# Row maxima of a graph attention layer: written to DRAM in two pieces, read back over 128 partitions, running maxima turned in contiguous blocks

## The chip, the cores and the metric

The kernel runs on one core of one Trainium2 chip. The metric is the device time of one execution in microseconds (us); lower is better.

## The reference, cut to what matters

For each of 8 graphs of N = 1500 nodes and 64 features, an attention layer with 4 heads comes first, and then three light layers with layer norms between them.

```
scores = einsum('hbnd,hbdm->hbnm', f_self, f_other)      # 4 heads, 1500 x 1500 each
masked = a * scores;  masked = where(masked >= 0, masked, 0.2 * masked) / sqrt(16)
masked = masked + where(a == 0, -1e9, 0)
attn   = softmax(masked, axis=-1)
x = layernorm(x + relu(attn @ feats + bias))
x = layernorm(x + (adj + I) @ x / degree)
x = layernorm(x + adj @ (x @ w2) + bias2)
t = adj @ x;  x = layernorm(x + where(t > 0.5, 1, 0))
```

The softmax over a row of 1500 needs the row's maximum before any of its exponentials can be taken. The change touches only how these maxima travel.

## The kernel before, in words

P = 125 nodes stand on the partitions, 12 tiles of them make the 1500. C = 500 is a slice of rows (ST = 4 nodes to a partition), and there are 3 slices. A unit is one graph, one pair of heads and one slice: 48 units, u = 0 to 47, six to a graph. A unit has 12 steps, one for each tile of 125 neighbours, so there are 576 steps q, and every engine runs through one loop over q in which each job has a fixed offset.

In step q, TensorE fills a PSUM tile Z (125 neighbours by 2 heads by 500 rows: two matmuls at L496 with the mask, two at L498 with the scores). ScalarE bends it with the leaky function into LS (L677). VectorE keeps the running maximum RUN over the steps (L820 in a unit's first step, L823 in the others). The neighbours lie on the partitions, so after 12 steps RUN still has 125 candidates for each of the 1000 maxima. One step later the unit's maxima are finished and spread, in this order:

1. TensorE transposes RUN in eight matmuls (turn_run, L509, one for each of 2 heads and 4 groups of 125 rows). PE's order in that step is fixed: the turn comes ahead of the next fill of Z.
2. VectorE reduces the turned tile to RMAX, 125 x 8 (row_maxima, L829).
3. ScalarE bends it into LMAX (L692).
4. The SyncE queue (SP) writes LMAX to a DRAM row of 1000 numbers, `spread` (the tensor row_maxima, L303), waits until that has landed, and reads the row back into MB on all 125 partitions (L309). MB and `spread` have two buffers each, for u even and odd. The same queue issues the feature copies (L286, 24 in a batch, two batches to a graph) and the loads and stores of x.

The subtraction of the maxima runs 18 steps behind the fill (LAG): POOL does two steps of three (L403), VectorE every third (L837), and POOL's first one of a unit waits for MB. POOL's next pair waits for VectorE's one. Two steps behind the subtraction ScalarE takes the exponential (L685), and two behind that TensorE multiplies by the values V (L535). LS holds 24 steps; the fill of a new one needs an old one to have been weighed.

Between these, in steps fixed by hand, stand the turns of the adjacency (L552: three transposes, each of a contiguous block of 125 words), the light layers of the graph before (L586 and L596 on TensorE, L905 to L940 on VectorE, L408 and L412 on POOL) and the features of the next one.

Of the kernel before, what the change touches and what calls it, by code (L numbers as in the profile page):

```python
# [8 lines left out]
P = 125  # L9
NT = N // P  # L10
ST = 4
NS = NT // ST
C = ST * P
# [55 lines left out]
def adj_resnorm(nc, x, adj, wv, wself, wother, bias0, w2, bias2, out):  # L69
    f32, bf16, f16, f8 = mybir.dt.float32, mybir.dt.bfloat16, mybir.dt.float16, mybir.dt.float8e4  # L70
    ALU, ACT, AX = mybir.AluOpType, mybir.ActivationFunctionType, mybir.AxisListType
# [6 lines left out]
    spread = nc.dram_tensor("row_maxima", (2, 2 * C), f32).ap()  # L78

    ctx = ExitStack()  # L80
    with ctx:
        def sb(name, shape, dt):
            return ctx.enter_context(nc.sbuf_tensor(name, shape, dt))

        def sem(name):
            return ctx.enter_context(nc.semaphore(name))
# [5 lines left out]
        LS = sb("LS", [128, RL, 2, C], f32)  # L92
        V = sb("V", [P, 2, NT, H, VC], f32)
        RUN = sb("RUN", [P, 2, 2, C], f32)
        MB = sb("MB", [P, 2, 2, C], f32)
        PARTS = sb("PARTS", [128, 3, N], bf16)
        YT = sb("YT", [128, C], f32)
        REST = sb("REST", [128, C], f32)
# [18 lines left out]
        LMAX = sb("LMAX", [P, 2, 2 * ST], f32)  # L117
# [5 lines left out]
        ID = sb("ID", [128, 128], f32)  # L123
# [23 lines left out]
        max_out = [sem(f"max_out{i}") for i in range(2)]  # L147
        mb_in = [sem(f"mb_in{i}") for i in range(2)]
        sub_pool = sem("sub_pool")
        sub_dve = sem("sub_dve")  # L150
# [49 lines left out]
        def unit_at(q, at):  # L200

            u, off = divmod(q - at, STEPS)
            return u if off == 0 and 0 <= u < NU else None

        def graph_at(q):
            return divmod(q, SPG)
# [60 lines left out]
        def banks(*what):  # L267
            return Z[:, place[what] % RZ, :, 0:C]

        def link_of(b, l, n):  # L270

            return LINKS * b + 3 * l + n + 1

        def by_pool(e):

            return e // TURN * (TURN - 1) + min(e % TURN, TURN - 1)


        @block.sync
        def _(sp):  # L280
            def load_rows(b, dst, sem_):
                sp.dma_start(dst.rearrange("p (s k) f -> p s k f", k=ST), x_v[b]).then_inc(sem_, 16)

            def load_parts(dst, sem_, side, h):
                for n, pair in enumerate(TERMS):
                    sp.dma_start(dst[n * D:(n + 1) * D],  # L286
                                 PARTS[side * F + h * D:side * F + (h + 1) * D, pair[side], :]).then_inc(sem_, 16)

            def load_features(b, p):
                sp.wait_ge(lo_ready, NS * (b + 1))  # L290
                if b >= 1:

                    sp.wait_ge(z_full, SPG * (b - 1) + NS * STEPS * (p + 1))
                for h in (2 * p, 2 * p + 1):
                    load_parts(FO[:, h, :], fo_in[p], 1, h)
                    load_parts(FS[:, h, :], fs_in[p], 0, h)

            def spread_maxima(u):
                sp.wait_ge(max_bent, u + 1)
                if u >= 2:  # L300

                    sp.wait_ge(mb_in[u % 2], 16 * (u // 2))
                sp.dma_start(spread[u % 2].rearrange("(h i c) -> i h c", i=P, c=ST),  # L303
                             LMAX[:, u % 2, :].rearrange("p (h c) -> p h c", c=ST)).then_inc(max_out[u % 2], 16)
                sp.wait_ge(max_out[u % 2], 16 * (u // 2 + 1))
                if u >= 2:
                    sp.wait_ge(sub_pool, by_pool(STEPS * (u - 1)))
                    sp.wait_ge(sub_dve, STEPS * (u - 1) // TURN)
                sp.dma_start(MB[:, u % 2, :, :].rearrange("p h c -> p (h c)"),  # L309
                             spread[u % 2].partition_broadcast(P)).then_inc(mb_in[u % 2], 16)  # L310

            load_rows(0, XF, xf_in)
            sp.dma_start(WA[:, 0, :, :], wself.rearrange("h f o -> f h o")).then_inc(early_in, 16)
            sp.dma_start(WA[:, 1, :, :], wother.rearrange("h f o -> f h o")).then_inc(early_in, 16)
            sp.dma_start(WV[:, :, :], wv.rearrange("h f o -> f h o")).then_inc(early_in, 16)
            load_features(0, 0)
            load_features(0, 1)
            sp.dma_start(WW[0:F, 1, :], w2).then_inc(weights_in, 16)
            sp.dma_start(WW[F:2 * F, 1, :], w2).then_inc(weights_in, 16)
            sp.dma_start(B0[:, :, :].rearrange("p h o -> p (h o)"),  # L320
                         bias0.rearrange("a b h o -> (a b h o)").partition_broadcast(P)).then_inc(weights_in, 16)
            sp.dma_start(B2[:, :], bias2.partition_broadcast(P)).then_inc(weights_in, 16)
            load_rows(0, XA[:, :, :], xa_in)
            for q in range(END):
                b, r = graph_at(q)
                if unit_at(q, MAX_AT) is not None:
                    spread_maxima(unit_at(q, MAX_AT))
                if r == 1 and 1 <= b < B:
                    load_features(b, 1)
                if r == 11 and b + 1 < B:  # L330
                    if b >= 2:

                        sp.wait_ge(dve_seq, link_of(b - 2, 3, 2))
                    load_rows(b + 1, XF, xf_in)
                if r == 13 and b >= 2:
                    sp.wait_ge(x_ready, 4 * (b - 1))
                    sp.dma_start(out_v[b - 2], X[:, :, :].rearrange("p (s k) f -> p s k f", k=ST)).then_inc(stored, 16)
                if r == 29 and 1 <= b < B:
                    sp.wait_ge(dve_seq, link_of(b - 1, 0, 1))
                    load_rows(b, XA[:, :, :], xa_in)  # L340
                if r == 37 and b + 1 < B:
                    load_features(b + 1, 0)
            for c in range(NS):
                sp.wait_ge(end_x, 9 + c + 1)
                sp.dma_start(out_v[B - 1][:, c], X[:, ST * c:ST * (c + 1), :]).then_inc(stored, 16)
            for p in range(PAIRS):
                sp.wait_ge(fs_in[p], 16 * 2 * NF * B)
                sp.wait_ge(fo_in[p], 16 * 2 * NF * B)
            sp.wait_ge(stored, 16 * (B - 1) + 16 * NS)
# [3 lines left out]
        def _(pool):  # L353
# [40 lines left out]
            def subtract(e):  # L394
                u, c = divmod(e, STEPS)
                if c == 0:
                    pool.wait_ge(mb_in[u % 2], 16 * (u // 2 + 1))
                if e % TURN == 0:

                    pool.wait_ge(sub_dve, e // TURN)  # L400
                pool.wait_ge(bent, e + 1)
                rows = LS[:P, e % RL, :, :]
                nc.gpsimd.tensor_tensor(rows, rows, MB[:, u % 2, :, :], ALU.subtract).then_inc(sub_pool, 1)  # L403

            def power(b, l):

# [57 lines left out]
        def _(pe):  # L464
# [37 lines left out]
            def turn_run(u):  # L502

                pe.wait_ge(maxed, STEPS * (u + 1))
                ring_free(place["RT", u])
                z = banks("RT", u)
                for hh in range(2):
                    for c in range(ST):
                        last = nc.tensor.transpose(z[:P, hh, c * P:(c + 1) * P], RUN[:, u % 2, hh, c:C:ST], ID[:P, :P])  # L509
                last.then_inc(run_turned, 1)  # L510

            def degrees(u):
# [137 lines left out]
            for l in range(3):  # L650
                for q in range(NS):
                    pe.wait_ge(end_low, 3 * l + q + 1)
                    for c in range(NS):
                        if l and q == 0:
                            pe.wait_ge(end_taken, 3 * (l - 1) + c + 1)
                        for m in range(ST * q, ST * (q + 1)):
                            last = nc.tensor.matmul(Z[:, c, 0, 0:C], XP[:, m, :], AT[:P, (NS * (B - 1) + c) % RS, q, :, m % ST],  # L657
                                                    start=(m == 0), stop=(m == NT - 1))
                        if q == NS - 1:
                            last.then_inc(end_y, 1)  # L660
                for c in range(NS):
# [3 lines left out]
                    for k in range(ST):  # L665
                        last = nc.tensor.matmul(Z[:P, c, 1, k * F:(k + 1) * F], parts[c][:, k * P:(k + 1) * P],
                                                WW[:, 1 if l == 1 else 0, :], start=True, stop=True)
# [4 lines left out]
        def _(act):  # L672
# [14 lines left out]
            def bend_maxima(u):  # L687

                act.wait_ge(max_found, u + 1)
                if u >= 2:  # L690
                    act.wait_ge(max_out[u % 2], 16 * (u // 2))
                nc.scalar.activation(LMAX[:, u % 2, :], RMAX[:, u % 2, :], ACT.Prelu, alpha=0.2).then_inc(max_bent, 1)  # L692

            def take(u):
# [109 lines left out]
        def _(dve):  # L804
# [28 lines left out]
            def subtract(e):  # L833
                u, c = divmod(e, STEPS)
                dve.wait_ge(mb_in[u % 2], 16 * (u // 2 + 1))
                rows = LS[:P, e % RL, :, :]
                nc.vector.tensor_tensor(rows, rows, MB[:, u % 2, :, :], ALU.subtract).then_inc(sub_dve, 1)  # L837

            def keep_adj(g, k, bank):
                dve.wait_ge(a_turned, ST * g + k + 1)  # L840
# [108 lines left out]
            for q in range(END):  # L949
# [12 lines left out]
                if feature_at(q) and feature_at(q)[0] == "FT":  # L962
                    _, bb, c = feature_at(q)
# [16 lines left out]
                if 0 <= e < QN and e % TURN == TURN - 1:  # L980
                    subtract(e)
# [99 lines left out]
```

## Time and profile before

| | |
|---|---|
| median of 3 runs | 1768.12 us (1765.34 to 1771.2) |
| the profiled execution's own time | 1762.62 us |
| its span | 1760.8 us |
| mean granted TensorE clock | 0.912 |
| busy: PE, DVE, ACT, POOL | 1454.2, 1384.5, 1241.6, 1089.5 us |

The span runs from the first to the last instruction of the profiled execution. PE is TensorE's matmuls and PEld its weight loads, DVE is VectorE, ACT ScalarE, POOL GpSimd, SP SyncE. A busy share is not a bound by itself: the engines hand tiles to one another, and the chain of waits tells which work stood last at each moment.

### The profile page before, as it was taken

What the parts mean: (1) busy time and instruction counts of PE and PEld (TensorE: products, weight loads), DVE (VectorE), ACT (ScalarE), POOL (GpSimd) and SP (SyncE); (2) the same over time, 40 slices, a digit from 0 to 9 for tenths busy, and PEclk for the clock granted to TensorE, in tenths of its full rate; (3) what the DMA queues carried; (4) which work ended last, traced back from release to release, by engine and by line L of the source; (5) the groups of instructions that cost most, each with busy time, mean ns of one, the idle gap of its engine ahead of it and who ended that gap; (6) DMA issues with size and microseconds to landing.
All of it is one profiled execution on the core that took longest, in us unless ns stands there. A gap on an engine that the chain in (4) does not pass through costs nothing.

```text
span 1760.8 us, 22052 instructions
## 1 busy us (share of the span) xinstructions
PE 1454.2 (83%) x7728; PEld 718.8 (41%) x7728; DVE 1384.5 (79%) x1623; ACT 1241.6 (71%) x1475; POOL 1089.5 (62%) x581
## 2 busy tenths in 40 slices
PE   4487889898889889888889888988899987888745
PEld 3233334444444444444444443444444443344313
DVE  3567788878898778888888778987888788888654
ACT  2377878777687777777787777777687777777521
POOL 1056676676676666676576667776666766766642
PEclk9788989999899999999999999999999999999767
DMA  5413142122413133221522234130432214000000
GB/s 77 61 32 48 31 66 40 46 30 39 70 31 46 26 52 51 52 36 26 68 40 43 25 55 58 39 44 17 63 46 52 30 37 55 21 12 24 15 6 9
DMA packets 55067, 71.42 MB, mean 41 GB/s; under 512 B 21814, under 2 KB 42814, under 8 KB 54958
## 3 DMA queue, kind: packets, MB, share of 16 engines
q0 software_dynamic: 13824, 18.01, 13.7%
q1 hardware_dynamic: 41134, 52.01, 11.4%
q8 instruction: 62, 1.02, 0.3%
q14 instruction: 47, 0.39, 0.1%
HBM read 102.29 MB, written 3.26 MB: 60 GB/s over the span
## 4 chain that ended last, share of the span: by engine, by line
PE 45%; DVE 24%; issue 12%; ACT 11%; SPq 3%; POOL 3%; DMA 2%; ACTq 0%; POOLq 0%; DVEq 0%
PE M L586 11%; DVE RUN L823 9%; PE M L535 9%; PE Z L496 8%; PE Z L498 7%; ACT LS L677 6%; PE Z L509 4%; DVE LS L837 4%; ACT LS L685 3%; SPq L286 2%; DVE X L922 2%; POOL LS L403 2%; PE Z L596 2%; DVE RUN L820 2%; PE Z L657 2%
## 5 line engine op out<-in xcount | busy, mean ns | idle before, releaser
L403 POOL TENSOR_TENSOR LS<-LS,MB 125x1000 f32<-125x1000 f32 x384 | 894.7, 2346 | 489.4 <-DVE LS L837 334.8
L823 DVE TENSOR_TENSOR RUN<-Z,RUN 125x1000 f32<-125x1000 f32 x528 | 631.0, 1195 | 208.7 <-ACT LS L677 203.4
L677 ACT ACTIVATE LS<-Z 125x1000 f32<-125x1000 f32 x576 | 574.5, 998 | 262.0 <-PE Z L498 261.4
L685 ACT ACTIVATE LS<-LS 125x1000 f32<-125x1000 f32 x576 | 594.5, 1033 | 71.3 <-POOL LS L403 56.2
L496 PE MATMUL Z<-AT,BI 126*125 126x500 fp8e4 x1152 | 386.0, 418 | 140.1 <-DVE RUN L823 107.0
L535 PE MATMUL M<-LS,V 125*18 125x500 f32 x2304 | 326.7, 642 | 57.8 <-ACT LS L685 57.0
L498 PE MATMUL Z<-FS,FO 96*125 96x500 bf16 x1152 | 360.1, 395 | 0.0
L837 DVE TENSOR_TENSOR LS<-LS,MB 125x1000 f32<-125x1000 f32 x192 | 283.2, 1475 | 4.9 <-DMA MB<-row_maxima 2.8
L496 PEld LDWEIGHTS Z<-AT,BI 126*125 126x125 bf16 x1152 | 140.7, 146 | 282.9 <-DVE RUN L823 164.5
L498 PEld LDWEIGHTS Z<-FS,FO 96*125 96x125 bf16 x1152 | 165.5, 144 | 111.4 <-issue 21.3
L586 PE MATMUL M<-AT,XP 125*128 125x500 fp8e4 x756 | 206.8, 396 | 0.7 <-ACTq L735 0.7
L586 PEld LDWEIGHTS M<-AT,XP 125*128 125x128 f16 x756 | 63.6, 98 | 169.6 <-issue 106.8
L509 PE MATMUL Z<-ID,RUN 125*125 125x125 f32 x384 | 99.9, 407 | 26.8 <-DVE RUN L820 24.1
L535 PEld LDWEIGHTS M<-LS,V 125*18 125x18 f32 x2304 | 39.6, 98 | 185.4 <-issue 101.7
L509 PEld LDWEIGHTS Z<-ID,RUN 125*125 125x125 f32 x384 | 91.5, 323 | 46.3 <-DVE RUN L820 39.9
L365 POOL DMA_DIRECT2D A<-in_adj_dram x96 | 53.7, 560 | 85.9 <-PE Z L552 58.7
L820 DVE TENSOR_SCALAR RUN<-Z 125x1000 f32<-125x1000 f32 x48 | 57.3, 1193 | 47.8 <-DMA B<-in_L_gnn_bias_dram 30.0
L829 DVE TENSOR_REDUCE RMAX<-Z 125x8 f32<-125x1000 f32 x48 | 57.3, 1194 | 26.1 <-PE Z L509 26.1
L596 PEld LDWEIGHTS Z<-WW,YT 128*125 128x125 f32 x504 | 63.9, 190 | 28.7 <-issue 22.0
L922 DVE SCALAR_TENSOR_TENSOR X<-Y,RSTD 125x768 f32<-125x768 f32 x28 | 72.4, 2585 | 3.6 <-POOL RSTD L408 2.4
L596 PE MATMUL Z<-WW,YT 128*125 128x64 f32 x504 | 64.7, 272 | 3.7 <-DVE RUN L820 3.7
L552 PEld LDWEIGHTS Z<-ID,A 125*125 125x125 f32 x276 | 45.8, 215 | 53.5 <-issue 28.5
(118 smaller groups left out, 1039.6 us busy)
## 6 DMA issues: line engine op xcount, KB each, us to landing
MB<-row_maxima SPq DMA_DIRECT2D x48, 488.3 KB
A<-in_adj_dram POOLq DMA_DIRECT2D x96, 183.1 KB, 4.8
FO<-PARTS SPq DMA_DIRECT2D x192, 46.9 KB, 2.1
FS<-PARTS SPq DMA_DIRECT2D x192, 46.9 KB, 2.1
XP<-in_x_dram SPq DMA_DIRECT2D x8, 375.0 KB
XA<-in_x_dram SPq DMA_DIRECT2D x8, 375.0 KB
out_dram<-X SPq DMA_DIRECT2D x7, 375.0 KB
row_maxima<-LMAX SPq DMA_DIRECT2D x48, 3.9 KB
```

The source lines that it names most:

```text
L403: nc.gpsimd.tensor_tensor(rows, rows, MB[:, u % 2, :, :], ALU.subtract).then_inc(sub_pool, 1)
L496: nc.tensor.matmul(z[:P, hh, :], BI[:, :], AT[:, g % RS, quarter, :, k], start=True, stop=False)
L498: last = nc.tensor.matmul(z[:P, hh, :], FO[:, 2 * p + hh, m * P:(m + 1) * P], FS[:, 2 * p + hh, s * C:(s + 1) * C], start=False, stop=True)
L509: last = nc.tensor.transpose(z[:P, hh, c * P:(c + 1) * P], RUN[:, u % 2, hh, c:C:ST], ID[:P, :P])
L535: last = nc.tensor.matmul(M0[VW * n:VW * n + VC, 0:C], V[:, b % 2, e % STEPS, 2 * p + hh, :], LS[:P, e % RL, hh, :], start=(p == 1 and j = ...
L586: last = nc.tensor.matmul(M1[:, 0:C], XP[:, m, :], AT[:P, (NS * b + c) % RS, m // ST, :, m % ST], start=(m == 0), stop=(m == NT - 1))
L596: last = nc.tensor.matmul(z[:P, 0, k * F:(k + 1) * F], YT[:, k * P:(k + 1) * P], WW[:, 1 if l == 1 else 0, :], start=True, stop=True)
L677: nc.scalar.activation(LS[:P, q % RL, :, :], banks("Z", q)[:P], ACT.Prelu, alpha=0.2).then_inc(bent, 1)
L685: nc.scalar.activation(rows, rows, ACT.Exp, scale=0.25).then_inc(exps, 1)
L823: nc.vector.tensor_tensor(run, z, run, ALU.max).then_inc(maxed, 1)
L837: nc.vector.tensor_tensor(rows, rows, MB[:, u % 2, :, :], ALU.subtract).then_inc(sub_dve, 1)
L922: nc.vector.scalar_tensor_tensor(out=X[:, :, :], in0=Y[:, :, :], scalar=F ** 0.5, in1=RSTD[:, :].unsqueeze(2).to_broadcast(bc3), op0=ALU.m ...
```

## The change

The running maxima are turned in blocks of 125 neighbouring columns, where before each transpose took every fourth column. The results in PSUM then belong to rows c * 125 + i instead of 4 * i + c, and the write to DRAM puts them back in order: it goes number by number. It is issued in two DMAs, of partitions 0 to 111 and 112 to 124. The read back fills 128 partitions of MB, of which 125 are used as before. The waits on the write's semaphore count 32 for each unit where they counted 16.

```diff
-        MB = sb("MB", [P, 2, 2, C], f32)
+        MB = sb("MB", [128, 2, 2, C], f32)
...
-                sp.dma_start(spread[u % 2].rearrange("(h i c) -> i h c", i=P, c=ST),
-                             LMAX[:, u % 2, :].rearrange("p (h c) -> p h c", c=ST)).then_inc(max_out[u % 2], 16)
-                sp.wait_ge(max_out[u % 2], 16 * (u // 2 + 1))
+
+                for rows in (slice(0, 112), slice(112, P)):
+                    sp.dma_start(spread[u % 2].rearrange("(j i) -> i j", i=P)[rows], LMAX[rows, u % 2, :],
+                                 allow_slow_non_contiguous=True).then_inc(max_out[u % 2], 16)
+                sp.wait_ge(max_out[u % 2], 32 * (u // 2 + 1))
...
                 sp.dma_start(MB[:, u % 2, :, :].rearrange("p h c -> p (h c)"),
-                             spread[u % 2].partition_broadcast(P)).then_inc(mb_in[u % 2], 16)
+                             spread[u % 2].partition_broadcast(128)).then_inc(mb_in[u % 2], 16)
...
-                nc.gpsimd.tensor_tensor(rows, rows, MB[:, u % 2, :, :], ALU.subtract).then_inc(sub_pool, 1)
+                nc.gpsimd.tensor_tensor(rows, rows, MB[:P, u % 2, :, :], ALU.subtract).then_inc(sub_pool, 1)
...
-                        last = nc.tensor.transpose(z[:P, hh, c * P:(c + 1) * P], RUN[:, u % 2, hh, c:C:ST], ID[:P, :P])
+                        last = nc.tensor.transpose(z[:P, hh, c * P:(c + 1) * P], RUN[:, u % 2, hh, c * P:(c + 1) * P], ID[:P, :P])
...
-                    act.wait_ge(max_out[u % 2], 16 * (u // 2))
+                    act.wait_ge(max_out[u % 2], 32 * (u // 2))
```

## Rows read from the trace of the kernel before

**Rows 1.** The page's busy tenths in 40 slices of the span.

```profile
PE   4487889898889889888889888988899987888745
DVE  3567788878898778888888778987888788888654
PEclk9788989999899999999999999999999999999767
```

**Rows 2.** The chain that ended last, shares of the span by line.

```profile
by line: issue 12.2%; PE M L586 10.6%; DVE RUN L823 8.9%; PE M L535 8.6%; PE Z L496 7.7%; PE Z L498 6.7%; ACT LS L677 5.7%; PE Z L509 4.5%; DVE LS L837 4.0%; ACT LS L685 3.0%; SPq L286 2.5%; DVE X L922 2.4%; POOL LS L403 2.2%; PE Z L596 2.1
```

**Rows 3.** Turns in the timeline of PE: start us, us, instructions.

```profile
834.92 2.04 PE L509 MATMUL Z<-ID,RUN 125*125 125x125 f32 x8
801.39 2.17 PE L509 MATMUL Z<-ID,RUN 125*125 125x125 f32 x8 [0.32 <-DVE XA L867]
67.05 0.49 PE L552 MATMUL Z<-ID,A 125*125 125x125 f32 x3
63.59 0.84 PE L552 MATMUL Z<-ID,A 125*125 125x125 f32 x3
```

**Rows 4.** Weight loads and matmuls of two lines: duration ns min/median/max.

```profile
L509 PEld LDWEIGHTS Z<-ID,RUN x384: 302/325/327, 80.7 to 1643.8; 125*125 125x125 f32 x192
L552 PEld LDWEIGHTS Z<-ID,A x276: 183/188/336, 63.2 to 1493.6; 125*125 125x125 f32 x138
L552 PE MATMUL Z<-ID,A x276: 267/273/571, 63.6 to 1493.7; 125*125 125x125 f32 x138
```

**Rows 5.** Groups of instructions: busy us, mean ns, idle before and its releaser.

```profile
L403 POOL TENSOR_TENSOR LS<-LS,MB 125x1000 f32<-125x1000 f32 x384 | 894.7, 2346 | 489.4 <-DVE LS L837 334.8 <-DMA MB<-row_maxima 150.6 <-ACT LS L677 3.8
L685 ACT ACTIVATE LS<-LS 125x1000 f32<-125x1000 f32 x576 | 594.5, 1033 | 71.3 <-POOL LS L403 56.2 <-DVE LS L837 2.8
L837 DVE TENSOR_TENSOR LS<-LS,MB 125x1000 f32<-125x1000 f32 x192 | 283.2, 1475 | 4.9 <-DMA MB<-row_maxima 2.8
```

**Rows 6.** Who waited for whom, SP's queue and POOL: total us, times, longest us.

```profile
SPq L309 <- DMA row_maxima<-LMAX: 96.4, 48, 3.3
POOL LS L403 <- DMA MB<-row_maxima: 150.6, 34, 9.8
```

**Rows 7.** SP's issues, durations in ns min/median/max, and L286's landing.

```profile
L303 SPq DMA_DIRECT2D row_maxima<-LMAX x48: 251/252/431, 85.7 to 1647.1; - x48
L309 SPq DMA_DIRECT2D MB<-row_maxima x48: 259/260/267, 89.0 to 1649.2; - x48
L286 SPq DMA_DIRECT2D FS<-PARTS x192: 576/589/1857, 25.0 to 1451.7; - x192
```

**Rows 8.** The page's hardware DMA queue: packets, MB, share of 16 engines' span.

```profile
q1 hardware_dynamic: 41134, 52.01, 11.4%
```

**Rows 9.** Windows: us, busy of five engines, PEclk, DMA share, GB/s.

```profile
607.00:611.00 4.00, 3.19 (x24) 1.06 (x16) 3.85 (x5) 3.99 (x5) 3.89 (x3) 1.00 0.27 104
```

**Rows 10.** Timeline of SP, then of POOL, unit 14.

```profile
541.30 0.27 SPq L309 DMA_DIRECT2D MB<-row_maxima  x1
...
547.96 4.61 POOL L403 TENSOR_TENSOR LS<-LS,MB 125x1000 f32<-125x1000 f32 x2 [5.38 <-DMA MB<-row_maxima]
```

**Rows 11.** The chain in order of time, units 0, 2, 5 and 11: start us, us.

```profile
88.99 9.28 DMA MB<-row_maxima
...
153.54 7.61 issue
...
241.26 8.81 DMA MB<-row_maxima
...
449.78 2.41 issue
452.19 3.29 DVE LS L837
```

**Rows 12.** Timeline around the first subtractions of unit 11.

```profile
449.15 5.27 POOL L403 TENSOR_TENSOR LS<-LS,MB 125x1000 f32<-125x1000 f32 x2 [7.39 <-DMA MB<-row_maxima]
...
451.49 1.04 ACT L685 ACTIVATE LS<-LS 125x1000 f32<-125x1000 f32 x1 [3.00 <-POOL LS L403]
```

More of the change, by code:

```diff
@@ L836, in subtract @@
                 rows = LS[:P, e % RL, :, :]
-                nc.vector.tensor_tensor(rows, rows, MB[:, u % 2, :, :], ALU.subtract).then_inc(sub_dve, 1)
+                nc.vector.tensor_tensor(rows, rows, MB[:P, u % 2, :, :], ALU.subtract).then_inc(sub_dve, 1)
             def keep_adj(g, k, bank):
```

## The prediction, made before the changed kernel ran

> **What bounds the kernel now.** I read the page first. PE is busy in eight or nine tenths of nearly every slice and DVE in seven or eight [rows 1], so no engine is the bound alone. The chain of waits tells more: it passes through PE's matmuls, DVE's running maxima and ACT's steps in turn, and L509, the turn of RUN, holds 4.5% of the span in it [rows 2]. That is 0.045 x 1760.8 = 79 us, and at about 1.9 us a turn it is 41 of the 48 turns: nearly each one stands where nothing else can go on. Then I looked for the other half of the change, the way of the maxima through DRAM. POOL waits for MB 150.6 us in 34 of 48 units [rows 5, 6]. POOL has slack, so this is not a gain by itself; it becomes one where ACT's exponential then waits for POOL (56.2 us in all) [rows 5], and in a few places of the chain [rows 11].
>
> **The turn.** Eight transposes stay eight; only the operand's step changes. Today each weight load of L509 lasts 302 to 327 ns at any clock, while L552's, the same 125 x 125 f32 from neighbouring words, lasts 188 in the median [rows 4]. The load sets the pace: eight turns last 2.04 us at the full clock [rows 3], so with a last matmul of some 0.3 us the step between two is 0.25. L552's three last 0.49 us at the full clock; less one matmul of 0.27 [rows 4] that is 0.11 us a step, and eight would last 0.27 + 7 x 0.11 = 1.04 us. That saves 1.0 us a turn. At the low clock L552's three last 0.84 us, which gives 0.21 a step and some 1.9 us for eight, against the 2.17 of a turn in which the clock fell [rows 3]: 0.3 saved. PEclk is 9 in most slices [rows 1], and nearly all turns start at the full clock with about a quarter ending at the low one, so I take 0.9. On the chain this is 41 x 0.9 = 37 us. L829 (RMAX), the next fill of Z (L496) and everything behind them come that much sooner. Bounds: nothing, if the f32 transpose were paced otherwise, and 1.0 x 48 = 48 us.
>
> **The read back.** How many DMA engines carry MB? The window of unit 16 in which only MB moves shows a DMA share of 0.27 at 104 GB/s [rows 9], near 5/16. The packets say the same. Of the 41,134 on the hardware queue [rows 8] the shapes of its transfers explain 34,290 (12,000 of the maxima's write, 6,000 of MB, 6,144 feature rows, 9,000 of x in and out, 1,146 of weights and biases). The other 6,844 are one completion for each engine used, and that comes out exactly with 5 engines for the 124 transfers over 125 rows and 16 for the 389 over 16 or 64 rows: 620 + 6,224. So 125 rows go on five engines, and 128 should go on 16, as every row count divisible by 16 here does. The Trainium skill says so too (DMA: Bandwidth & Descriptors, Why a DMA increments its semaphore by 16 and not by 1): the engines are the largest number up to 16 that divides the slowest dimension, which gives 5 for 125, 16 for 128 and 112, and 13 for 13; by this count the trace agrees for 125, 16 and 64. The same page (Specifications) puts the DRAM limit of one core near 358 GB/s; by it the read would take 1.4 us, so that limit would not change the sum.
>
> The 500 KB now take 500,000 / 104,000 = 4.8 us. With each of 16 engines at the rate of the five, 333 GB/s, the 512 KB take 1.5 us: 3.3 saved. The other end is no gain: all 16 read the same 4 KB of DRAM, and no row shows more than this rate from one such place. I take 3.3, because the engines' rate looks like their own. Against that stands the issue: SP needs 0.26 us for L309 but 0.59 for a feature copy on 16 engines [rows 7], so +0.33.
>
> **The write.** Today 250 pieces of 16 bytes go out; after, 1000 of 4 bytes: 896 / 16 = 56 an engine and then 8 more, against 50 now. If a small packet costs the same, the transfer lasts as long as now. The issues are two of 0.59 instead of one of 0.25 [rows 7]: the second ends at 1.2 us after the first began, where today's ends at 0.25, so the landing comes 0.8 to 0.9 later (less than the difference, since the first piece is under way by then). SP's wait for the write is 96.4 / 48 = 2.0 us now [rows 6] and should read some 2 from the last issue. Bounds: below, +0.3; above, each of the 64 packets at the queue's mean, 0.114 x 16 x 1760.8 us / 41,134 = 0.078 us [rows 8], or 5.0 us, +5.5 with the issue. I take +0.8: today's 50 packets and their receipt fit into 2.0 us together, so a small one costs far less than the mean. SP's queue carries 1.3 us more issue a unit, 60 us in all, in a queue that is mostly waiting; the feature batches it delays by that are issued many steps ahead of their use, so this costs nothing unless a batch runs straight into a spread, where it is in the sum already.
>
> **When POOL starts.** The parts add up to -3.3 + 0.33 + 0.8 = -2.2 us from LMAX to MB, and -3.2 with the turn's 1.0. In unit 14 POOL starts 6.7 us after L309's issue [rows 10]; that should become some 3.7 (6.7 - 3.3 + 0.33). What is late next is POOL's own work: its last subtraction of the unit before, or DVE's, which frees its next pair (334.8 us of POOL's idle time are due to that [rows 5]).
>
> What of it is on the chain? I find eight places: units 0, 2 and 5 [rows 11], and the pattern of unit 11, which comes again in 29, 35, 41 and 47. In unit 11 POOL gets MB at 449.15, so that ACT waits 3.00 us for the first subtraction [rows 12] and DVE's own L837 stands in the chain after 2.41 us of nothing, lasting 3.29 us [rows 11] where its mean is 1.475 [rows 5]: it meets POOL's second subtraction. The turn's 1.0 moves all of this together, so only the 2.2 counts: 8 x 2.2 = 18 us. For the other forty units, where the chain shows no such piece, I add nothing.
>
> **The sum.** 37 + 18 = 55 us is what the chain could give. As each piece goes, another engine stands within a fraction of a us of it (DVE and PE are both near eight tenths busy [rows 1]), so I keep four fifths: 44 us. The profiled execution took 1762.6 us, which becomes 1718.6; its median stands 5.5 us above that one (1768.1), so I predict 1724 us. The remaining edits cost nothing: MB on three more partitions is the same instruction for POOL and DVE (still 125 rows), and the doubled semaphore counts add no wait.
>
> **The rivals.**
>
> *Only the turn pays (0.17).* The read of one 4 KB place does not scale to 16 engines, or the write takes what the read gives. For it: no row shows this rate; against it: the five engines show no sign of waiting for one another. Then 18 falls out: 37 x 0.8 = 30, so 1738 us.
>
> *Only the read pays (0.08).* DVE or ACT takes the turn's place in the chain at once. For it: DVE's eight tenths; against it: on PE's side the next fill of Z stands directly behind the turn. 1768 - 18 = 1750 us.
>
> *The write becomes the bound, and the kernel slower (0.07).* 1000 writes of 4 bytes, of which different engines hit neighbouring words of the same DRAM row, may cost more each. Each us by which MB comes later than today delays POOL in the 34 units in which it already waits, and ACT in most of them, some 40 us in all at 1 us over all 48. The turn's 30 us cover 0.8 us of that. So it decides from a write stage that is 2.2 + 1.0 + 0.8 = 4 us longer than my +0.8, or 4 / 64 = 62 ns a small packet beyond today's; the upper bound above, +5.5, lies just past that. At 1 us beyond it, 1768 + 40 = 1808 us. The Trainium skill speaks for this rival (DMA: Bandwidth & Descriptors, Specifications): below 512 bytes the DMA engine does a read-modify-write. But by that rule today's 16-byte pieces pay it too, within the 2.0 us, so I leave the chance low.
>
> *The clock takes it back (0.05).* PE's work shrinks by 3% (48 of 1454 us), and what PE does at the low clock costs up to 0.84 / 0.49 = 1.7 times as much [rows 3]. For it: PEclk dips wherever PE stalls [rows 1]; against it: with shorter waits it should stall less. If the low stretches grow enough to eat the gain, 1766 us, no change.
>
> **How the numbers follow.** The forecast as it stands has 0.63: 1724 us, on its own 1708 to 1742 (the turn's 37 whole or half, the read's 18 whole or nothing). For 8 times in 10 the range must take in the second case and most of the third: 1704 to 1750. Between two builds of this kernel less than 0.3% (5 us) can't be told from no change. Faster: 0.63 + 0.17 + 0.07 = 0.87, the third case giving most of its 0.08. Same: 0.06. Slower: 0.07.
>
> **What would show it right or wrong.** In the profile after: L509's loads at some 190 ns and eight turns in 1.0 to 1.1 us at the full clock; L509's share of the chain down from 4.5% to about 2.5%; three DMA issues a unit at about 0.6 us each on SP; a DMA share near 0.8 in the microsecond or two in which MB moves; POOL starting some 3.7 us after the read's issue, and its total wait for MB falling from 150.6 us to some 60; ACT's wait for POOL falling from 56 us to under 35. SP's wait for the write is the test of the fourth case: at 2 to 3 us from the first issue I am right, above 6 us I am wrong. I would also be wrong if packets of MB lasted three times as long on 16 engines, or if DVE's subtractions met POOL's in new places: L837's mean would rise above 1475 ns.

## The result, and the profile after

The changed kernel takes 1862.84 us (median of 4 runs) against 1768.03 us: a ratio of 1.054 with a 95% interval of 1.0489 to 1.0591. It is 95 us slower where I had forecast 44 us faster, and it lies outside the range of 1704 to 1750. The profiled execution was a disturbed one (1885.39 us, clock 0.875, where the undisturbed ones show 0.882 to 0.889), so below I use its waits and durations and not its span.

The groups that answer to those of before; columns as in [rows 5], the turn's as in [rows 4]:

```profile
L405 POOL TENSOR_TENSOR LS<-LS,MB 125x1000 f32<-125x1000 f32 x384 | 916.9, 2406 | 587.9 <-DMA MB<-row_maxima 294.7
L687 ACT ACTIVATE LS<-LS 125x1000 f32<-125x1000 f32 x576 | 594.3, 1033 | 220.2 <-POOL LS L405 205.6
L839 DVE TENSOR_TENSOR LS<-LS,MB 125x1000 f32<-125x1000 f32 x192 | 307.0, 1599 | 38.1 <-DMA MB<-row_maxima 35.9
```

```profile
L511 PEld LDWEIGHTS Z<-ID,RUN x384: 182/189/336, 80.8 to 1762.7; 125*125 125x125 f32 x192
L511 PE MATMUL Z<-ID,RUN x384: 270/273/573, 81.0 to 1762.8; 125*125 125x125 f32 x192
```

The turn did what it should: a load lasts 189 ns instead of 325 in the median [rows 4]. But POOL's wait for MB rose from 150.6 to 294.7 us [rows 5], and ACT's wait for POOL from 56.2 to 205.6 us. So MB comes later, not sooner. The next three answers tell which part of its way is to blame: SP's waits (as in [rows 6]), the read's issue and landing, and the chain by line (as in [rows 2]).

```profile
SPq L311 <- DMA row_maxima<-LMAX: 360.1, 48, 12.2
```

```profile
L311 SPq DMA_DIRECT2D MB<-row_maxima x48: 337/338/352, 94.9 to 1774.0; - x48
...
DMA to landing us min/median/max: 3.7/4.7/8.3
```

```profile
by line: issue 17.1%; POOL LS L405 9.4%; DMA row_maxima<-LMAX 7.2%; SPq L286 6.1%; DVE RUN L825 6.0%; ACT LS L679 5.3%; PE Z L498 4.9%; PE M L537 4.7%; PE Z L500 4.1%; PE M L588 4.1%; DMA MB<-row_maxima 3.9%; ACT LS L687 3.4%; DVE X L924 2.
```

SP waits 360.1 / 48 = 7.5 us a unit for the write, from its last issue on, where it waited 2.0 [rows 6]. The write now holds 7.2% of the chain, a line that [rows 2] did not show at all, and the turn has left the part of the line that is shown. The read is quicker than it was: it lands a median 4.7 us after its issue, and in unit 14 POOL starts 4.2 us after it (591.19 to 595.39 below), where it took 6.7 [rows 10] and I had said 3.7.

```profile
591.19 0.34 SPq L311 DMA_DIRECT2D MB<-row_maxima  x1
...
595.39 5.55 POOL L405 TENSOR_TENSOR LS<-LS,MB 125x1000 f32<-125x1000 f32 x2 [10.59 <-DMA MB<-row_maxima]
```

Where do 7.5 us go? Unit 1 shows it, in SP's timeline and then in windows (columns as in [rows 9]):

```profile
120.69 0.88 SPq L305 DMA_DIRECT2D row_maxima<-LMAX  x2
129.24 0.34 SPq L311 DMA_DIRECT2D MB<-row_maxima  x1
```

```profile
120.50:123.00 2.50, 1.70 (x8) 0.81 (x6) 2.50 (x3) 2.38 (x5) 0.86 (x1) 1.00 0.20 2
123.00:129.00 6.00, 5.61 (x33) 2.28 (x33) 4.31 (x6) 6.00 (x9) 3.74 (x2) 1.00 0.00 0
```

Both issues are out at 121.6 and their packets are gone before 123. Then for 6 us the DMA engines do nothing (share 0.00), and only at 129.2 does SP hear that the write has landed. The packets are as cheap as I had assumed: by the trace's packet records one lasts a median 9 ns, at 16 bytes before and at 4 bytes now. What costs comes behind them: from the end of the last packet to the read's issue it is a mean 0.9 us before and 5.7 us now.

The mean of 7.5 us hides two sizes. In 13 units the write stands directly behind a batch of feature copies in SP's queue. Six of these (11, 17, 23, 29, 35 and 41) wait 9.4 to 12.3 us; the other 42 units wait a mean of 7.0. The chain shows one of the six:

```profile
465.57 0.59 SPq L286
...
466.26 0.53 SPq L305
466.79 0.04 issue
466.83 11.74 DMA row_maxima<-LMAX
```

In the 13 units SP is also late for the write itself: LMAX has been ready for 2.5 to 5.4 us while SP still issues a batch (in 14 units before, for 1.1 to 5.2 us).

### The profile page after: what moved, and what is told of

The parts are those of the page before. It is cut to its first block, busy times and chain, and to the rows that moved or that the text cites. A ratio compares the mean times of both kernels' runs of the same rounds, so it can differ in the third digit from the quotient of the medians.

```text
span 1883.6 us, 22100 instructions
## 1 busy us (share of the span) xinstructions
PE 1463.5 (78%) x7728; PEld 694.1 (37%) x7728; DVE 1405.7 (75%) x1623; ACT 1243.2 (66%) x1475; POOL 1112.2 (59%) x581
## 3 DMA queue, kind: packets, MB, share of 16 engines
q1 hardware_dynamic: 78958, 52.60, 13.7%
## 4 chain that ended last, share of the span: by engine, by line
PE 26%; DVE 18%; issue 17%; DMA 12%; ACT 11%; POOL 10%; SPq 7%; ACTq 0%; POOLq 0%; DVEq 0%
POOL LS L405 9%; DMA row_maxima<-LMAX 7%; SPq L286 6%; DVE RUN L825 6%; ACT LS L679 5%; PE Z L498 5%; PE M L537 5%; PE Z L500 4%; PE M L588 4%; DMA MB<-row_maxima 4%; ACT LS L687 3%; DVE X L924 2%; DVE LS L839 2%; DVE RUN L822 2%; PE Z L659 2%
## 5 line engine op out<-in xcount | busy, mean ns | idle before, releaser
L405 POOL TENSOR_TENSOR LS<-LS,MB 125x1000 f32<-125x1000 f32 x384 | 916.9, 2406 | 587.9 <-DMA MB<-row_maxima 294.7
L825 DVE TENSOR_TENSOR RUN<-Z,RUN 125x1000 f32<-125x1000 f32 x528 | 631.6, 1196 | 282.6 <-ACT LS L679 275.8
L687 ACT ACTIVATE LS<-LS 125x1000 f32<-125x1000 f32 x576 | 594.3, 1033 | 220.2 <-POOL LS L405 205.6
L498 PE MATMUL Z<-AT,BI 126*125 126x500 fp8e4 x1152 | 393.9, 425 | 177.1 <-DVE RUN L825 143.5
L537 PE MATMUL M<-LS,V 125*18 125x500 f32 x2304 | 335.3, 657 | 71.2 <-ACT LS L687 69.4
L500 PE MATMUL Z<-FS,FO 96*125 96x500 bf16 x1152 | 364.7, 400 | 0.0
L839 DVE TENSOR_TENSOR LS<-LS,MB 125x1000 f32<-125x1000 f32 x192 | 307.0, 1599 | 38.1 <-DMA MB<-row_maxima 35.9
L521 PE MATMUL M<-AT,DS 125*18 125x500 fp8e4 x288 | 29.0, 524 | 85.2 <-ACT O L700 85.2
L511 PE MATMUL Z<-ID,RUN 125*125 125x125 f32 x384 | 61.5, 310 | 27.0 <-DVE RUN L822 24.6
L511 PEld LDWEIGHTS Z<-ID,RUN 125*125 125x125 f32 x384 | 52.9, 214 | 46.6 <-DVE RUN L822 39.2
```

Of the source, the lines that this page charges most:

```text
L405: nc.gpsimd.tensor_tensor(rows, rows, MB[:P, u % 2, :, :], ALU.subtract).then_inc(sub_pool, 1)
L498: nc.tensor.matmul(z[:P, hh, :], BI[:, :], AT[:, g % RS, quarter, :, k], start=True, stop=False)
L500: last = nc.tensor.matmul(z[:P, hh, :], FO[:, 2 * p + hh, m * P:(m + 1) * P], FS[:, 2 * p + hh, s * C:(s + 1) * C], start=False, stop=True)
L537: last = nc.tensor.matmul(M0[VW * n:VW * n + VC, 0:C], V[:, b % 2, e % STEPS, 2 * p + hh, :], LS[:P, e % RL, hh, :], start=(p == 1 and j = ...
L687: nc.scalar.activation(rows, rows, ACT.Exp, scale=0.25).then_inc(exps, 1)
L825: nc.vector.tensor_tensor(run, z, run, ALU.max).then_inc(maxed, 1)
```

## The experiments

The runs are grouped by the question that they answer. Where maxima belong to other rows, or MB holds other numbers that are the same on every partition, the softmax is still the same up to rounding (it doesn't depend on what is subtracted from a row), but the safe range of its exponentials is lost, so these are for their time. In read_apart each partition subtracts numbers of its own, and there the results are wrong.

### The parts alone

turn_only:

```diff
-    last = nc.tensor.transpose(..., RUN[:, u % 2, hh, c:C:ST], ID[:P, :P])
+    last = nc.tensor.transpose(..., RUN[:, u % 2, hh, c * P:(c + 1) * P], ID[:P, :P])
```

> The turn alone: RUN is turned in contiguous blocks, the write and the read back are those of before (the maxima then belong to permuted rows, so this one is for its time only). Theory A, that the write's landing alone made the kernel slow: L509's eight last 1.1 us instead of 2.04 and the time falls by 20 to 35 us against before (ratio 0.980 to 0.989). Theory B, that the turn gives nothing since DVE or the clock takes its place: ratio 0.997 to 1.003.

Measured: 1751.53 us, ratio 0.9928 (0.9903 to 0.9953). Faster, but by 13 to 15 us (by the ratio and by the medians of its own set, 1766.07 us for before) instead of 20 to 35. The rows say where the rest went, the chain last:

```profile
POOL LS L403 <- DMA MB<-row_maxima: 170.8, 33, 9.0
ACT LS L685 <- POOL LS L403: 82.2, 41, 8.0
by line: issue 13.3%; DVE RUN L823 9.8%; PE M L586 8.7%; PE M L535 7.3%; PE Z L496 6.5%; SPq L286 5.8%; PE Z L498 5.7%; ACT LS L677 5.6%; DVE LS L837 3.5%; ACT LS L685 3.3%; DMA MB<-row_maxima 3.2%; POOL LS L403 3.0%; DVE RUN L820 2.1%; DVE
```

POOL's wait for MB grew by 20 us and ACT's for POOL by 26 us against [rows 5]. With PE quicker, more of the chain runs over the way of the maxima: DMA MB<-row_maxima holds 3.2% and SP's issuing of feature copies (L286) 5.8%, where [rows 2] had 2.5%. In 14 units SP comes to the write 2.5 to 5.7 us after LMAX is ready, since it is still issuing a batch; there a turn that ends sooner brings MB no sooner.

read128:

```diff
-        MB = sb("MB", [P, 2, 2, C], f32)
+        MB = sb("MB", [128, 2, 2, C], f32)
...
-                             spread[u % 2].partition_broadcast(P)).then_inc(mb_in[u % 2], 16)
+                             spread[u % 2].partition_broadcast(128)).then_inc(mb_in[u % 2], 16)
```

> The read back alone, over 128 partitions; turn and write as before. In the changed kernel the read took a median 4.7 us from issue to landing. Theory A: here it takes 4 to 5 us instead of 6.7, POOL's wait for MB falls from 150.6 us to 70 to 110, and the time falls by 5 to 15 us (ratio 0.991 to 0.997). Theory B, that reading one place with 16 engines gives nothing on the whole: ratio 0.998 to 1.003.

Measured: 1729.34 us, ratio 0.9797 (0.9772 to 0.9821), 36 us of gain and more than either theory gave. The read lands as theory A said:

```profile
L309 SPq DMA_DIRECT2D MB<-row_maxima x48: 336/343/351, 88.8 to 1613.5; - x48
...
DMA to landing us min/median/max: 3.6/4.2/8.2
```

POOL's wait for MB fell to 65.6 us, ACT's for POOL to 34.8 us.

write_only (the two DMAs of the change with their waits, on before):

```diff
-                sp.dma_start(spread[u % 2].rearrange("(h i c) -> i h c", i=P, c=ST),
-                             LMAX[:, u % 2, :].rearrange("p (h c) -> p h c", c=ST)).then_inc(max_out[u % 2], 16)
+                for rows in (slice(0, 112), slice(112, P)):
+                    sp.dma_start(spread[u % 2].rearrange("(j i) -> i j", i=P)[rows], LMAX[rows, u % 2, :],
+                                 allow_slow_non_contiguous=True).then_inc(max_out[u % 2], 16)
```

> The write alone, number by number and in 112 and 13 partitions; turn and read as before (permuted maxima, for its time only). Theory A: SP's wait for the write goes from 96.4 us to about 360, MB comes some 6.4 us later in each unit, and the time rises by more than that of the whole change: +110 to +160 us (ratio 1.062 to 1.09). Theory B, that the slowdown comes from the parts together (16 engines reading while adjacency loads run, other meetings of POOL and DVE): under +60 us.

Measured: 1981.39 us, ratio 1.1225 (1.1196 to 1.1254): 215 us slower, more than theory A's range, and theory B (under 60) is out. POOL now waits for MB in all 48 units, and ACT for POOL:

```profile
SPq L310 <- DMA row_maxima<-LMAX: 342.6, 48, 9.2
POOL LS L404 <- DMA MB<-row_maxima: 373.3, 48, 14.7
ACT LS L686 <- POOL LS L404: 296.1, 74, 13.1
```

turn_read (both edits above, before's write):

> Turn and read of the change, the write of before (permuted maxima, for its time only). Theory A: the two gains add up, 30 to 50 us less than before (ratio 0.972 to 0.983), which is what I had forecast for the whole. Theory B, that something in the turn or the read is itself harmful: ratio above 0.99.

Measured: 1702.41 us, ratio 0.9645 (0.9621 to 0.9669). The gain of 64 us is more than 13 and 36 together: on top of the quicker read the same turn gives about twice what it gives alone. So the turn and the read are good, and the changed kernel is this one plus 160 us for its write.

### What is slow in the write

write_one (one DMA of 125 partitions, 4-byte pieces):

```diff
-                for rows in (slice(0, 112), slice(112, P)):
-                    sp.dma_start(spread[u % 2].rearrange("(j i) -> i j", i=P)[rows], LMAX[rows, u % 2, :],
-                                 allow_slow_non_contiguous=True).then_inc(max_out[u % 2], 16)
+                sp.dma_start(spread[u % 2].rearrange("(j i) -> i j", i=P), LMAX[:, u % 2, :],
+                             allow_slow_non_contiguous=True).then_inc(max_out[u % 2], 16)
```

> The changed kernel, but the 1000 numbers go out in one DMA of 125 partitions (five engines, 200 pieces each) and not in two on 16 and 13. Count theory (each separate 4-byte piece has a price of its own where it lands): SP's wait for the write stays at 6 to 8 us a unit, since there are still 1000 pieces. Split theory (two DMAs or many engines at once are what is slow): 2 to 3 us a unit, 110 to 150 us in all.

write_split16 (before's turn and pieces, in two DMAs, read over 128):

```diff
+                for rows in (slice(0, 112), slice(112, P)):
+                    sp.dma_start(spread[u % 2].rearrange("(h i c) -> i h c", i=P, c=ST)[rows],
+                                 LMAX[rows, u % 2, :].rearrange("p (h c) -> p h c", c=ST)).then_inc(max_out[u % 2], 16)
```

> Before's turn and its 16-byte pieces (250), read over 128 partitions, but written in two DMAs of 112 and 13 partitions. Count theory: SP's wait for the write from its last issue is about 2 us a unit, 85 to 110 us in all, and the second issue adds some 0.5 us to the way. Split theory: 6 us or more a unit.

One run each beside one of before (1765.08 us): write_one 1808.39 us, write_split16 1728.34 us. SP's waits, write_one first:

```profile
SPq L310 <- DMA row_maxima<-LMAX: 329.7, 48, 9.7
```

```profile
SPq L310 <- DMA row_maxima<-LMAX: 76.2, 48, 4.7
```

6.9 us a unit with one DMA on five engines, 1.6 with two DMAs of 16-byte pieces. So neither the split nor the number of engines makes the wait long, and the small pieces do. The split theory is out (write_split16 takes 1728 us, and read128, the same kernel with one DMA, 1729). The single DMA still saves an issue: from the first issue to the read's it is a mean 7.3 us in write_one and 8.6 in the changed kernel, which goes with the some 50 us between their times. Yet "each piece has its price" was not true either, as the next two show:

write_lines (each partition's eight numbers in 64 bytes of their own):

```diff
+    apart = nc.dram_tensor("apart", (2, P * 8 * 2), f32).ap()
...
-                    sp.dma_start(spread[u % 2].rearrange("(j i) -> i j", i=P)[rows], LMAX[rows, u % 2, :],
+                    sp.dma_start(apart[u % 2].rearrange("(i j t) -> i j t", i=P, t=2)[rows, :, 0], LMAX[rows, u % 2, :],
...
-                             spread[u % 2].partition_broadcast(128)).then_inc(mb_in[u % 2], 16)
+                             adj[0, 0, 0:2 * C].partition_broadcast(128)).then_inc(mb_in[u % 2], 16)
```

> The changed kernel with its 1000 pieces of 4 bytes in two DMAs, but each partition's eight go to 64 bytes of their own in another DRAM row (8 bytes apart), so that no two partitions share such a stretch; MB is read from one row of the adjacency (values without meaning, for time only). Count theory: SP's wait stays at 6 to 8 us a unit. Neighbour theory (pieces of different engines in the same few bytes of DRAM hold one another up): 2 to 3 us a unit.

write_far (the same with `(j i t) -> i j t`, t=16: 64 bytes from number to number):

> As the one before, but every number goes 64 bytes away from the next: 1000 pieces spread over 64 KB. Count theory: 6 to 8 us a unit, perhaps more. Neighbour theory: 2 to 3 us a unit. If write_lines is slow and this one is fast, it is pieces meeting in one short stretch, whichever engine sends them.

write_lines took 1784.83 us, write_far 1713.09 us. SP's waits, in the same order:

```profile
SPq L312 <- DMA apart<-LMAX: 236.3, 48, 9.7
```

```profile
SPq L312 <- DMA apart<-LMAX: 118.4, 48, 5.7
```

write_far has the changed kernel's 1000 pieces, engines and issues, and waits 2.5 us a unit instead of 7.5. The count theory falls. write_lines waits 4.9 us, though no two partitions share its 64 bytes: so it needn't be different partitions that meet, as the neighbour theory had it. Pieces that fall close together in DRAM take longer to land, whoever sends them.

write_far3 is write_far in three rounds:

> write_far again, timed: 1000 pieces of 4 bytes with 64 bytes between them and the read over 128 partitions. By the neighbour theory it is faster than before, at 1705 to 1722 us (ratio 0.965 to 0.975), though it writes as many pieces on as many engines as the changed kernel.

Measured: 1714.73 us, ratio 0.9744 (0.9718 to 0.9771).

write_p2, write_p4 and write_p8 are write_far with t = 2, 4 and 8, one run each beside one of before (1768.47 us):

> write_far with 8 bytes from number to number instead of 64. If pieces within 64 bytes wait for one another in turn, 8 share a stretch where 16 do in the changed kernel: SP's wait for the write about 4.5 to 5.5 us a unit (write_lines, with 8 in 64 bytes, had 4.9). If the whole 4 KB matters and not the stretch, spreading over 8 KB gives about half of 7.5, 3.8 us.

> 16 bytes from number to number: 4 pieces in 64 bytes. Stretch of 64 bytes: about 3.2 to 3.8 us a unit. Stretch of 32 bytes or less: close to write_far's 2.4 (2 pieces in 32).

> 32 bytes from number to number. Stretch of 64 bytes: about 2.6 to 3.0 us a unit, a little above write_far. Stretch of 32 bytes or less: the same as write_far's 2.4 within its scatter.

| bytes from number to number | SP's wait, us | a unit | time, us |
|---|---|---|---|
| 4 (the changed kernel) | 360.1 | 7.5 | 1862.84 |
| 8 (write_p2) | 179.6 | 3.7 | 1742.99 |
| 16 (write_p4) | 131.5 | 2.7 | 1711.82 |
| 32 (write_p8) | 120.6 | 2.5 | 1716.36 |
| 64 (write_far) | 118.4 | 2.5 | 1713.09 |

The wait rises steeply with how densely the pieces lie, and next to nothing of the rise is left from 32 bytes on: turn_read, with 250 pieces of 16 bytes, waits 112.8 us in all. It is not in proportion. What stands above the last row's 2.5 us is 5.0, 1.3, 0.3 and 0.05 us a unit, about a quarter at each doubling. The packets have no part in it: from the last one's end to the read's issue the means are 5.7, 2.2, 1.4, 1.2 and 1.0 us. My numbers for a 64-byte stretch were too high for t = 2 (4.5 to 5.5 expected) and t = 4 (3.2 to 3.8); t = 2 fits the rival of half the wait over twice the room (3.8), but t = 4 and t = 8 do not go on halving. With 8 bytes between numbers the order in which they come matters as well: 4.9 us where one partition's eight follow one another (write_lines), 3.7 where neighbours are other partitions' numbers, over the same 8 KB. write_lines' two issues are longer too, a mean 1.5 us together against 1.0, so the wait from the last issue makes the difference look smaller than it is: behind the last packet it is 3.5 us against 2.2.

Three things stay open. Distance and the whole stretch (4 to 64 KB) grow together in the table, so it doesn't say which of the two sets the time. The first row writes the tensor that is read back and the others another one, and no run packs 4-byte pieces into that other tensor. And why six units are slower is not shown: write_far has the same six, at 4.5 to 5.8 us against a mean of 2.1 in the others.

### The read, and a version with everything in place

read_apart (turn_read with another source):

```diff
-                             spread[u % 2].partition_broadcast(128)).then_inc(mb_in[u % 2], 16)
+                             adj[0, 0:128, 0:2 * C]).then_inc(mb_in[u % 2], 16)
```

> Turn and read as in turn_read, but MB comes from 128 different rows of the adjacency and not from one place 128 times (values without meaning, for time only). Theory that one place of DRAM can't serve 16 engines: the read lands in 3.0 to 3.5 us instead of 4.2 and the time falls below turn_read's 1702 us by up to 10. Theory that a fixed start (each engine's first packet took about 0.9 us) and the packets' own 0.155 to 0.2 us make up the time: within 0.3 us of 4.2, the same time.

Measured: 1702.92 us, ratio 0.9679 (0.9657 to 0.9701), and the read lands in a median 3.7 us instead of 4.2. That is between the two theories; the kernel doesn't get faster by it. Nor is the 0.5 us the price of one place: write_far also reads one 4 KB place 128 times, of the adjacency, and its read lands in 3.7 us as well.

```profile
MB<-in_adj_dram SPq DMA_DIRECT2D x48, 500.0 KB, 3.7
```

The line is the same for read_apart and write_far. What differs in turn_read is the tensor read, which has just been written; the runs say no more on it.

blocks_z and blocks_run (turn and read of the change, before's write):

```diff
-                run, z = RUN[:, u % 2, :, :], banks("Z", q)[:P]
+                run = RUN[:, u % 2, :, :].rearrange("p h (c i) -> p h c i", c=ST)
+                z = banks("Z", q)[:P].rearrange("p h (i c) -> p h c i", c=ST)
```

> Both gains with the maxima in their right places: VectorE keeps RUN in four blocks of 125 and reads Z with a step of four words (the last loop runs over 125), so that the turn's operands are contiguous while the maxima still come out as 4 * i + c; the write is before's 16-byte one, the read goes over 128. If VectorE takes the steps for nothing (1195 ns for 1000 elements as now), the time is that of turn and read together, 1702 us, ratio 0.96 to 0.97. If a step of four words slows it, each of the 576 maxima lasts longer and the kernel ends at or above before: at twice the duration over 2000 us.

blocks_run has `p h i c` at the end of both lines:

> The same, but the last loop runs over the four blocks: Z is read in order and RUN with a step of 125 words. Either both versions take the same time (the element rate does not depend on the order), ratio 0.96 to 0.97, or this one is the cheaper or the dearer by what PSUM or SBUF asks for steps.

Measured: blocks_z 1702.45 us, ratio 0.9672 (0.9644 to 0.97); blocks_run 1885.86 us, ratio 1.0723 (1.0702 to 1.0744). VectorE's running maximum in before, in blocks_z and in blocks_run:

```profile
L823 DVE TENSOR_TENSOR RUN<-Z,RUN 125x1000 f32<-125x1000 f32 x528 | 631.0, 1195 | 208.7 <-ACT LS L677 203.4
```

```profile
L824 DVE TENSOR_TENSOR RUN<-Z,RUN 125x1000 f32<-125x1000 f32 x528 | 631.4, 1196 | 194.0 <-ACT LS L677 188.3
```

```profile
L824 DVE TENSOR_TENSOR RUN<-Z,RUN 125x1000 f32<-125x1000 f32 x528 | 1030.2, 1951 | 65.8 <-ACT LS L677 45.9 <-DVE RUN L824 1.0 <-DVE REST L876 0.2
```

So blocks_z beats both kernels, with every maximum belonging to its own row: the reordering happens in VectorE's reads of Z, where it costs nothing (1196 ns against 1195).

## Why the prediction was wrong, step by step

**The write: the step that failed.** I wrote "If a small packet costs the same, the transfer lasts as long as now" and took +0.8 us, with +5.5 as the upper end. The packets do cost the same: their engines are done within 2 us. The landing does not follow from the packets. My sign of being wrong was above 6 us from the first issue to the landing. From the first issue to the read's issue the mean grew from 2.4 to 8.6 us over the 48 units of the two traces (from the wait's 2.0 and 7.5 plus issue), +6.2, just past my upper end. Before's trace could not show this, as its 16-byte pieces wait 2.0 us in all; the mean price of a packet on the queue (0.078 us) came near the true size only by chance: one of these packets lasts 9 ns. That it is how densely the pieces lie in DRAM, and not count, engines or split, is shown by write_far, write_one and write_split16. What the memory does inside that time is not shown.

**What a late MB costs: right in price, wrong in its turning point.** My rival of this name set the turning point at 4.8 us of longer write and 40 us for each further one. By these a write 6.2 us longer costs 1.4 x 40 = 56 us over before; it cost 95. The price holds: write_only's +5.8 us, with nothing gained beside it, cost 215 us, which is 37 for each us over all 48 units. The turning point came sooner. Against turn_read's write, which takes 2.7 us from issue to issue:

| run | longer by, us | slower than turn_read (each against its own before), us |
|---|---|---|
| write_far | 0.8 | 12 |
| write_p2 | 2.1 | 38 |
| write_lines | 3.8 | 83 |
| write_one | 4.5 | 107 |
| after | 5.8 | 159 |

write_p2 is still faster than before and write_lines is not, so the 64 us that turn and read give are used up at about 3.1 us, which is 3.4 above before's write (all rows but the last are single runs). Past that point the price is mine again: 95 us for the last 2.7. One reason why it came sooner is that the read saves 2.5 us and not 3.0 (below); the rest of the difference is open. In 34 units POOL already waited for MB [rows 6]; I let all of them count for a loss, and for the gain only eight places of the chain. I gave this case 0.07.

**The turn** cost what I said: eight in 1.09 us at the full clock (1.04 expected; 2.04 in [rows 3]), in unit 14:

```profile
574.73 1.09 PE L511 MATMUL Z<-ID,RUN 125*125 125x125 f32 x8
```

But alone it gives 13 to 15 us, not 30. The chain's 79 us for L509 [rows 2] were not free to go, because the way of the maxima, and SP's batches in it, stood directly beside. The batches are a term that I put at nothing ("it is in the sum already"), and no piece of my sum has it: L286's share of the chain is 2.5% before and 6.1% in the changed kernel, 44 and 115 us.

**The read.** The engines are as counted. The changed kernel's hardware queue has 78,958 packets; its shapes explain 70,434, and the other 8,524 are 6,364 of the untouched transfers and 48 x (16 + 13 + 16). By the rule of the Trainium skill (DMA: Bandwidth & Descriptors, Why a DMA increments its semaphore by 16 and not by 1), the largest number up to 16 that divides the slowest dimension, the trace agrees for 128, 112 and 13 as well, as far as this count of completions tells. The size was off: I divided all of 4.8 us by the rate. In unit 1 of the changed kernel fifteen of MB's 128 packets, the first ones of their engines, last about 1.0 us and the others 0.155 to 0.23, and the first does not divide. (It varies: over all 48 transfers the median of the first 16 is 0.6 us in turn_read and 1.1 in the changed kernel, that of the others 0.155.) One transfer in a window of its own (columns as in [rows 9]):

```profile
130.20:132.80 2.60, 2.41 (x15) 0.88 (x15) 1.65 (x2) 2.48 (x4) 0.00 (x0) 1.00 0.79 197
```

512 KB in 2.6 us, not 1.5; the share is the 0.8 that I had said. From the read's issue to its last packet's end the median falls from 6.3 us before to 3.8 in read128, 2.5 saved where I had said 3.0, and in unit 14 POOL starts 4.2 us after the issue, not 3.7. Yet the read is worth more than I gave it: 36 us alone, against 18 x 0.8 = 14. Eight places at 2.5 us could not give that, so it pays in others of the 34 waits too.

**SP's issues** cost less than said: 0.3 and 0.5 us for the write, 0.34 for the read, not 0.59 each.

**The sum.** Without the write's 0.8 us my sum for turn and read would have been (37 + 8 x 3.0) x 0.8 = 49 us; they give 64. (In the second rival I took the read's 18 us whole, where the sum took four fifths of it; by that it is 1754 us and not 1750.) The sign came from the write alone. Of my other signs, POOL's total wait for MB and ACT's for POOL come to 80.5 and 33.0 us in turn_read, near the 60 and under the 35 that I gave. DVE's subtraction (L839) has a mean of 1599 ns, above the 1475 that I had named as a sign of being wrong. The clock (0.882 to 0.889, 0.912 before) fell as well, with PE waiting longer. It came down with the write, since turn_read, with the same PE work, has 0.926; what part of the 95 us it carries is not separated.

## What to carry to other kernels

When a change makes a DMA's pieces smaller, its price is not that of the packets: look at the wait of whoever needs the landing, and try the write alone before building on it. Numbers that must be reordered on their way are better reordered in an engine's access pattern, and in the operand where a step is free, than in DRAM. A buffer that a third engine already waits for in most rounds has little slack: here a us on its way was worth 0.3 us a round for the first ones (36 us for read128's 2.5 us, 12 for write_far's 0.8) and up to 0.8 when MB was late in every round (write_only). And look at what else the issuing queue carries directly ahead of the transfer that matters.

## What the runs showed of the hardware beyond that

- 1000 pieces of 4 bytes written to DRAM land a mean 2.5 us after the last issue with 32 or 64 bytes from one to the next (write_p8, write_far), 7.5 us when packed, with idle DMA engines in between. The Trainium skill (DMA: Bandwidth & Descriptors, Specifications) speaks of a read-modify-write below 512 bytes; the runs show that the size alone does not set the time.
- A VectorE maximum of 125 x 1000 f32 lasts 1196 ns with Z (PSUM) read in steps of 16 bytes and RUN (SBUF) in order, and 1951 ns with Z in order and RUN read and written in steps of 500 bytes.
- An f32 weight load of 125 x 125 from SBUF lasts 325 ns with steps of 16 bytes between words, whatever the granted clock, and 189 ns from neighbouring words at the full clock.
